# A megakernel of two transformer-like layers: 39 expert tiles, bias additions moved, the front of layer 1 a step sooner, the last quad in halves

## The chip, the cores and the metric

The kernel runs on one NeuronCore of one Trainium2 chip. The metric is the device time of one execution in microseconds; lower is better.

## The reference, cut to what matters

Two layers, each x + attention(xn) + ffn(xn), with xn the layer norm of x. x is 8 x 256 x 128 in float32, that is 2048 tokens in 16 tiles of 128.

```python
x = L0_attn_x
xn = _layernorm(x)
x = x + _L0_attn_ref(xn, ...) + _L0_ffn_ref(xn, ...)
xn = _layernorm(x)
x = x + _L1_attn_ref(xn, ...) + _L1_ffn_ref(xn, ...)
return x

# layer 0, attention: linear, 4 heads of 32
k = softmax(k, axis=1); context = einsum('bnhd,bnhe->bhde', k, v)
out = einsum('bhde,bnhd->bnhe', context, q) @ w_out + b_out; return out + x
# layer 0, ffn: 8 experts, each token goes to the best 2 by a router
h = u * silu(gate)          # [u, gate] = xn @ w_up[e].T, hidden 256
out = sum_k weight_k * (h_k @ w_down[e_k].T); return out + skip
# layer 1, attention: 16 heads of 64, q and k to unit length, 2 null keys,
# ALiBi slopes, causal mask, softmax; out @ w_out
# layer 1, ffn: 8 experts, grouped top 2 of a softmax router, hidden 256
```

## The kernel before

**Layer 0.** After the norms and the router, VectorE works out for each of the 4096 (token, expert) pairs a place in a list sorted by expert, each expert's part filled up to whole tiles of 128 places. At most 2 x 16 + 8 - 1 = 39 tiles are in use; the kernel handles 40 of them (`SLOTS`) in 20 pairs (`PAIRS`). `sources` turns the list into row numbers for the gathers, `slots` names each tile's expert. For each pair s, GpSimd issues two indirect DMAs (`pair_rows`, `sorted_tile`, line 505) into one of four rooms, so the gather of pair s waits for the transpose of pair s-4. TensorE's queue has, for each s in this order: the up products of pair s (six matmuls, lines 1483 to 1485, `pair_ups`), the transpose of the gathered rows of pair s+2 (`pair_turn`, line 1584), the down products of pair s-2 (line 1624), the transposes of the hidden rows of pair s-1 (line 1613). ScalarE and VectorE split the turned rows into a high and a low part, and do the gate. Between the gathers of pairs 5 to 8 and the next ones GpSimd does `output_bias`, an addition of the output bias to four tiles of the accumulator (line 500). SyncE stores each pair's results.

The attention of layer 0 is done by `mixing`, in ticks: in tick t the products of q and k of batch t, the rest of the batches before it. Ticks 0 to 5 stand behind the pairs, ticks 6 to 12 at steps of layer 1 listed in `MIX_AT` (line 383).

**Layer 1** is one sequence of steps s = -16 to 134, written out for each engine by `all_steps`. In step k (0 to 127) the scores of head pair k mod 8 of a query tile are computed (line 1812), biased on VectorE (line 1426), taken to the exponential on ScalarE (line 877); one step later the probabilities are turned (line 1876), three steps later multiplied with the values (line 1827). Four steps make a quad: a reciprocal and a product with it on VectorE (line 1412, `norm`), four transposes to `b_y` (line 1847), a copy (line 1468), eight passes of the output product (line 1798) and the addition to the accumulator (line 1449), at 7, 8, 8 and 10 steps behind the quad's first.

The `front` prepares q and k of the next batch in 8 pieces, two steps apart: projection (`PROJ_AT` = -9, lines 1483 to 1485, to the bank `b_front`), copy and square on ScalarE (lines 801, 805), sum on VectorE (line 1362, at -8), root on GpSimd (line 577, at -7), product with the root (line 318, -6, on VectorE for batches 0 and 7), transposes back to `b_front` (line 1690, `TURN_AT` = -4), copy on ScalarE (line 817). The scores of step 0 wait for two turned pieces.

`x1(b)` adds the rows that the experts of layer 0 gave (fetched by `take_rows(b)`, four gathers on GpSimd, line 544) to batch b's accumulator (line 1206) and takes the statistics, `row_roots` (line 552) their root on GpSimd, `x1_normal` and `x1_rhos` what follows on VectorE. For batch 1: x1 at step -5, root at -4, the rest at 1; `take_rows(2)` stands at step 0, `take_rows(3)` at step 3.

Each engine takes its instructions in order; a wait on a semaphore holds up all that is behind it on its engine.

## Time and profile before

| | |
|---|---|
| median of 3 runs | 642.15 us (641.12 to 643.76) |
| the profiled execution, its own time | 641.26 us |
| its span, first to last instruction | 639.4 us |
| TensorE matmul busy | 560.4 us, 88% of the span |
| ScalarE / VectorE / GpSimd busy | 432.4 / 423.9 / 351.1 us |
| mean granted TensorE clock | 0.983 of full |

The profile gives for each engine its busy time; a timeline of instructions with start, duration, line, operation, tiles written and read, and in brackets how long the engine was idle before and what released it; and tables of busy time for stretches of the span, with the clock that TensorE was granted (1.00 is 2.4 GHz, 0.50 is 1.2 GHz). Rough stages: norms, router and sorting until 44 us; expert pairs 44 to 120; mixing and the opening of layer 1 until 158; steps of layer 1 until 628; tail.

### The profile page before, as it was taken

How to read it: one execution, taken by the hardware profiler on the slowest of the kernel's cores; microseconds unless marked ns; L12 is line 12 of the kernel's file. 1: busy time of each engine (PE TensorE's matmuls, PEld its weight loads, DVE VectorE, ACT ScalarE, POOL GpSimd, SP SyncE). 2: the span in 40 equal slices, each digit the busy share in tenths (PEclk: the TensorE clock that was granted, in tenths of full speed). 3: DMA queues.
4: the chain of work that ended last, by engine and by line, in shares of the span. 5: the costliest groups of instructions: out<-in, count | busy, mean ns of one | idle time of the engine just before them, and what ended most of it. 6: DMA issues, size and time to landing. Idle time of an engine off the chain costs nothing.

```text
span 639.4 us, 13356 instructions
## 1 busy us (share of the span) xinstructions
PE 560.4 (88%) x3760; PEld 440.5 (69%) x3760; DVE 423.9 (66%) x1531; ACT 432.4 (68%) x1200; POOL 351.1 (55%) x302
## 2 busy tenths in 40 slices
PE   2417899986999988898999999999999999999797
PEld 1406688774767767666777777777777777777576
DVE  5785855475788776889756665566565665587663
ACT  3724786444877878676677777777777776887552
POOL 3617874235888696435564634554454443688800
PEclk9999999997799999999999999999999999999898
DMA  8602234410111013000000100100011100112200
GB/s 309 221 8 55 69 94 75 140 59 1 34 34 30 6 34 100 0 2 2 14 17 27 26 23 22 29 23 22 23 30 30 22 14 10 30 51 58 64 5 10
DMA packets 26326, 29.13 MB, mean 46 GB/s; under 512 B 3920, under 2 KB 22384, under 8 KB 25744
## 3 DMA queue, kind: packets, MB, share of 16 engines
q1 hardware_dynamic: 21680, 18.89, 9.4%
q0 software_dynamic: 4576, 9.38, 6.5%
q8 instruction: 35, 0.57, 0.4%
q14 instruction: 35, 0.29, 0.1%
HBM read 19.94 MB, written 8.32 MB: 44 GB/s over the span
## 4 chain that ended last, share of the span: by engine, by line
PE 58%; DVE 17%; POOL 11%; issue 9%; ACT 3%; DMA 2%; SPq 0%; POOLq 0%; DVEq 0%; ACTq 0%
PE b_last L1827 8%; PE b_upB L1812 7%; POOL taken L628 4%; PE b_rest L1876 4%; PE b_upB L1798 4%; PE b_last L1690 3%; PE b_rest L1665 3%; POOL moe_buf L505 3%; PE b_last L1483 2%; PE b_upA L1745 2%; PE b_upA L1483 2%; POOL rn L577 2%; PE b_rest L1847 2%; PE b_rest L1624 2%; PE b_upA L1484 2%
## 5 line engine op out<-in xcount | busy, mean ns | idle before, releaser
L877 ACT ACTIVATE prb<-prb,mneg 128x130 f32<-128x130 f32 (+1 forms) x256 | 114.7, 449 | 93.6 <-DVE mneg L1426 93.1
L577 POOL TENSOR_TENSOR rn<-ss,halves 128x8 f32<-128x8 f32 x64 | 107.4, 1679 | 97.0 <-DVE ss L1364 96.3
L1426 DVE CUSTOM_DVE_ANT_0 prb<-b_upB,bias 128x130 f32<-128x130 f32 (+1 forms) x256 | 81.5, 356 | 113.7 <-PE b_upB L1812 113.4
L505 POOL DMA_INDIRECT moe_buf<-normal_rows,source x79 | 79.7, 1009 | 93.1 <-PE b_rest L1779 62.9
L1827 PEld LDWEIGHTS b_last<-v,prT_all 128*128 128x128 f32 x768 | 100.1, 192 | 15.1 <-DVE qs_all L1412 8.7
L1827 PE MATMUL b_last<-v,prT_all 128*128 128x64 f32 x768 | 101.5, 268 | 5.6 <-DVE qs_all L1412 5.6
L1812 PE MATMUL b_upB<-qkT 64*128 64x258 f32 (+1 forms) x512 | 78.2, 383 | 0.2 <-DVE pnT L1436 0.2
L886 ACT ACTIVATE prT_all<-b_rest 128x512 f32<-128x512 f32 (+1 forms) x128 | 61.3, 479 | 6.8 <-PE b_rest L1876 6.2
L1876 PE MATMUL b_rest<-cst,prb 128*128 128x128 f32 x384 | 63.5, 274 | 0.0
L1876 PEld LDWEIGHTS b_rest<-cst,prb 128*128 128x128 f32 x384 | 47.7, 150 | 17.7 <-issue 17.6
L1812 PEld LDWEIGHTS b_upB<-qkT 64*128 64x128 f32 x512 | 39.4, 188 | 23.6 <-issue 18.5
L318 POOL TENSOR_TENSOR qk<-qk,rn 128x512 f32<-128x512 f32 x48 | 50.8, 1059 | 3.8
L877 ACT ACTIVATION_READ_ACCUMULATOR prb<-prb,mneg 128x1 f32 x256 | 47.8, 187 | 0.0
L1690 PE MATMUL b_last<-cst,qk 128*128 128x128 f32 x256 | 43.6, 295 | 3.9 <-DVE qk L318 3.0
L1362 DVE TENSOR_REDUCE ss<-sq 128x8 f32<-128x512 f32 x64 | 43.3, 676 | 4.0 <-ACT sq L805 3.7
L544 POOL DMA_INDIRECT taken<-expert_rows,pos x32 | 31.6, 988 | 22.4 <-DMA expert_rows<-moe_buf 13.9
L1798 PE MATMUL b_upB<-wout,oT 128*128 128x128 f32 x256 | 36.0, 285 | 6.8 <-DVE mneg L1426 6.0
L805 ACT ACTIVATE sq<-qk 128x512 f32<-128x512 f32 x64 | 40.4, 631 | 2.1
L1690 PEld LDWEIGHTS b_last<-cst,qk 128*128 128x128 f32 x256 | 28.5, 146 | 17.8 <-issue 7.8
L801 ACT ACTIVATE qk<-b_last 128x512 f32<-128x512 f32 x64 | 37.0, 577 | 4.6 <-PE b_last L1485 4.6
L1798 PEld LDWEIGHTS b_upB<-wout,oT 128*128 128x128 f32 x256 | 31.8, 196 | 9.4 <-issue 8.8
L628 POOL DMA_INDIRECT taken<-expert_rows,pos x32 | 33.1, 1033 | 8.8 <-issue 8.8
(330 smaller groups left out, 1272.2 us busy)
## 6 DMA issues: line engine op xcount, KB each, us to landing
expert_rows<-moe_buf SPq DMA_DIRECT2D x20, 128.0 KB, 1.9
expert_rows<-moe_buf SPq DMA_DIRECT2D x39, 64.0 KB, 1.5
bias<-w_up SPq DMA_DIRECT2D x1, 2048.0 KB, 9.5
down<-w_dn SPq DMA_DIRECT2D x2, 1024.0 KB, 10.6
moe_buf<-w_up SPq DMA_DIRECT2D x4, 512.0 KB, 4.1
moe_buf<-normal_rows,source POOLq DMA_INDIRECT x79, 2.6
qk<-x SPq DMA_DIRECT2D x8, 128.0 KB, 4.1
v<-w_qk SPq DMA_DIRECT2D x1, 1024.0 KB, 12.2
```

Source lines behind the costliest of these rows:

```text
L318: engine.tensor_tensor(part, part, norms.unsqueeze(2).to_broadcast([P, HALF, DH1]), ALU.mult).then_inc(unit, 1)
L505: nc.gpsimd.indirect_dma_start(out=room, out_offset=None, in_=normal_rows[layer], in_offset=bass.IndirectOffsetOnAxis(ap=source[layer][:, ...
L577: nc.gpsimd.tensor_tensor(rn[hs], ss[hs], halves[:], ALU.pow).then_inc(pool_root, 1)
L628: nc.gpsimd.indirect_dma_start(out=taken_rows[b % 2][:, t, k], out_offset=None, in_=expert_rows, in_offset=bass.IndirectOffsetOnAxis(ap=po ...
L877: nc.scalar.activation(prb[k % 3][:, i, 0:n], prb[k % 3][:, i, 0:n], ACT.Exp, scale=-1.0, bias=mneg[:, qt, h:h + 1], accum_out=lsum[:, qt, ...
L886: nc.scalar.activation(prT[k % 3][:, :, 0:n], b_prT[:, 0:2 * n].rearrange("p (a n) -> p a n", a=2), ACT.Copy).then_inc(act_prT, 1)
L1426: nc.vector.tensor_tensor_reduce(prb[k % 3][:, i, 0:n], b_sim[i][:, 0:n], bias[:, h, KEYS - n:KEYS], 1.0, FMAX, ALU.add, ALU.min, mneg[:, ...
L1690: ins = nc.tensor.transpose(b_front[:, i * P:(i + 1) * P], qk[:, w, t, hp * P:(hp + 1) * P], ident)
L1798: ins = nc.tensor.matmul(b_op, oT[:, a], wout1[:, m % 2 * 4 + a], start=(a == 0), stop=(a == 3))
L1812: nc.tensor.matmul(b_sim[i][:, 0:n], qT[ch, hp, toks], kT[ch, hp, 0:n], start=True, stop=True).then_inc(pe_sim, 1)
L1827: ins = nc.tensor.matmul(b_pv[:, at:at + DH1], prT[k % 3][:, i, c * P:(c + 1) * P], v[:, c, h * DH1:(h + 1) * DH1], start=(k % 4 == 0 and ...
L1876: ins = nc.tensor.transpose(b_prT[:, (i * nc1 + c) * P:(i * nc1 + c + 1) * P], prb[k % 3][:, i, NULL + c * P:NULL + (c + 1) * P], ident)
```

## The change

1. Layer 0 handles 39 tiles: the last pair has one tile in its gather, its transpose, its up, hidden and down work on TensorE. Operations of ScalarE and VectorE still treat both halves.
2. `output_bias` stands behind all gathers on GpSimd. `sources` stands ahead of `slots` on VectorE.
3. TensorE's turn of pair 1 stands behind the up products of pair 0.
4. In layer 1 the first four turns of the front go to the bank `b_pv` a step sooner, and don't wait for the projections; projections up to piece 6 don't wait for a turn's copy. Mixing ticks 9 to 12 stand at steps -7, -6, -5, -4 instead of -9, -8, -7, -6. For batch 1, x1 stands at step 1, its root at 2, the rest at 3.
5. Last quad (31): product, transposes and copy in two halves each, the second half turned to `b_front`. Quad 30: transposes at 7 instead of 8 steps behind, output product at 11 instead of 10.

```diff
+        EARLY_TURNS = 4
+        def turn_bank(m):
+            return b_pv if m < EARLY_TURNS else b_front
+        def turned_at(s):
+            return [m for m in piece_at(s, TURN_AT) if m >= EARLY_TURNS] + [m for m in piece_at(s, TURN_AT - 1) if m < EARLY_TURNS]
+        LAST = 4 * B - 1
+        def outputs_at(s):
+            return [m for m in quad_at(s, 8) if m != LAST - 1] + [m for m in quad_at(s, 7) if m == LAST - 1]
+        def projected_at(s):
+            return [m for m in quad_at(s, 10) if m != LAST - 1] + [m for m in quad_at(s, 11) if m == LAST - 1]
+        def turned_bank(a, m):
+            return b_y if m < LAST else (b_front if a else b_y)[:, 0:2 * P]
+        def parts_out(m):
+            return [(0, 2), (2, 4)] if m == LAST else [(0, 4)]
...
-        MIX_AT = [-STEPS, -11, -10, -9, -8, -7, -6]
+        MIX_AT = [-16, -11, -10, -7, -6, -5, -4]
...
+        def parts_of(s):
+            return range(2 if s < PAIRS - 1 else 1)
...
-                for t in range(2):
+                for t in parts_of(s):
                     sorted_tile(0, s, 2 * s + t, rows_in[s % 4][:, t], rows_loaded[s % 4])
...
                 pair_rows(s)
-                if 5 <= s < 9:
-                    output_bias(4 * (s - 5))
...
+            for at in range(0, TILES, 4):
+                output_bias(at)
...
-                if s == -4:
-                    row_roots(1)
...
+                if s == 2:
+                    row_roots(1)
...
+            sources(0)
             slots(0)
-            sources(0)
...
-                if s == -5:
+                if s == 1:
                     x1(1)
                     x1_variances(1)
-                if s == 1:
+                if s == 3:
                     x1_rhos(1)
                     x1_normal(1)
...
+                    for a, e in parts_out(m):
+                        cols_of, heads = slice(a * P, e * P), slice(2 * a, 2 * e)
+                        nc.vector.tensor_tensor(o_half[m % 2][:, cols_of]...,
+                                                b_pv[:, cols_of]...,
+                                                heads8[:, heads]..., ALU.mult).then_inc(dve_norm, 1)
...
-            pe.wait_ge(*ROUTED("source"))
+            pe.wait_ge(*ROUTED("slots"))
             load_experts(0)
...
-            for s in range(2):
-                pair_turn(s)
+            pair_turn(0)
             for s in range(PAIRS + 2):
                 if s < PAIRS:
                     pair_ups(s)
+                if s == 0:
+                    pair_turn(1)
...
-                    if m > 2:
+                    if m > EARLY_TURNS + 2:
                         pe.wait_ge(act_turn, m - 2)
...
-                    pe.wait_ge(act_proj, min(m + 3, 8 * B))
+                    if m == 0:
+                        pe.wait_ge(mix_dve["add"], mix_bank.index(b_pv) + 1)
+                    elif m >= EARLY_TURNS:
+                        pe.wait_ge(act_proj, min(m + 3, 8 * B))
```

## Rows read from the trace of the kernel before

**Rows 1.** Windows: stretch, length, busy of PE, PEld, DVE, ACT, POOL, granted clock, DMA.
```profile
440.00:460.00 20.00, 20.00 (x146) 16.27 (x145) 12.38 (x45) 15.20 (x45) 8.40 (x8) 1.00 0.09 22
149.00:155.00 6.00, 2.30 (x10) 1.09 (x8) 5.46 (x18) 3.35 (x6) 3.47 (x3) 0.84 0.00 0
...
161.00:164.00 3.00, 2.81 (x11) 1.78 (x9) 2.41 (x13) 2.05 (x7) 2.67 (x3) 0.50 0.26 67
...
167.00:170.00 3.00, 3.00 (x24) 2.36 (x22) 1.11 (x7) 2.67 (x8) 2.39 (x3) 1.00 0.18 44
```

**Rows 2.** Timeline (start, duration, engine, line, operation, idle before), TensorE in the pairs.
```profile
61.95 0.38 PE L1584 MATMUL b_last<-cst,moe_buf 128*128 128x128 f32 x2
...
73.95 0.44 PE L1584 MATMUL b_last<-cst,moe_buf 128*128 128x128 f32 x2 [1.19 <-DMA moe_buf<-normal_rows,source]
...
87.32 0.38 PE L1584 MATMUL b_last<-cst,moe_buf 128*128 128x128 f32 x2
...
104.78 0.40 PE L1485 MATMUL b_upA<-up_h,xa_l 128*128 x1
105.02 0.38 PE L1584 MATMUL b_last<-cst,moe_buf 128*128 128x128 f32 x2
105.24 1.06 PE L1624 MATMUL b_rest<-down,moe_buf 128*128 x8
```

**Rows 3.** Timeline, GpSimd in the pairs: bias addition, gathers, the operation behind the gathers.
```profile
59.55 1.29 POOL L500 TENSOR_TENSOR acc_all<-acc_all,small 128x512 f32<-128x512 f32 x1
...
68.38 1.77 POOL L505 DMA_INDIRECT moe_buf<-normal_rows,source  x1 [0.16 <-issue]
70.45 0.94 POOL L505 DMA_INDIRECT moe_buf<-normal_rows,source  x1 [0.30 <-issue]
...
106.19 2.38 POOL L532 TENSOR_TENSOR nvbd<-taken,nvbd 16x1024 fp32r<-16x1024 f32 x1 [4.35 <-issue]
```

**Rows 4.** Timeline, the last source matmul and the source cast.
```profile
42.27 0.32 PE L1560 MATMUL b_rest<-moe_buf,th 128*128 128x40 f16 x4 [0.29 <-DVE th L1055]
...
43.25 0.18 DVE L1065 CAST source<-b_rest 128x40 uint32<-128x40 f32 x1
```

**Rows 5.** Timeline, VectorE beside bias additions and without one.
```profile
66.85 2.46 DVE L1142 TENSOR_TENSOR wqk_l<-v,wqk_h 128x1024 fp32r<-128x1024 f32 x1
...
71.60 0.69 DVE L1173 TENSOR_TENSOR th<-b_upB,th 128x512 f32<-128x512 f32 x1
...
72.53 1.27 DVE L1142 TENSOR_TENSOR wqk_l<-v,wqk_h 128x1024 fp32r<-128x1024 f32 x1
```

**Rows 6.** Timeline, the opening: x1 of batch 1, turn 1, projection 4, first scores.
```profile
151.13 1.25 DVE L1206 SCALAR_TENSOR_TENSOR acc_all<-taken,half_share,acc_all 128x128 f32<-128x128 f32 x4
...
155.05 1.08 PE L1690 MATMUL b_last<-cst,qk 128*128 128x128 f32 x4 [1.60 <-DVE qk L318]
...
157.01 0.76 PE L1483 MATMUL b_last<-wqk_h,xa_h 128*128 128x512 f32 x1 [0.87 <-ACT qkT L817]
...
158.55 0.81 PE L1812 MATMUL b_upB<-qkT 64*128 64x130 f32 x4
```

**Rows 7.** Timeline, GpSimd in the first steps of layer 1.
```profile
158.17 1.02 POOL L544 DMA_INDIRECT taken<-expert_rows,pos  x1 [0.17 <-issue]
...
162.98 1.68 POOL L577 TENSOR_TENSOR rn<-ss,halves 128x8 f32<-128x8 f32 x1
...
166.24 1.46 POOL L544 DMA_INDIRECT taken<-expert_rows,pos  x1 [0.30 <-issue]
```

**Rows 8.** Timeline, the tail: output products, product with the reciprocals, last addition.
```profile
630.12 1.11 PE L1798 MATMUL b_upB<-wout,oT 128*128 128x128 f32 x8
...
632.45 0.69 DVE L1412 TENSOR_TENSOR qs_all<-b_last,rl 128x512 f32<-128x512 f32 x1 [0.79 <-DVE rl L1407]
...
634.69 2.04 PE L1798 MATMUL b_upB<-wout,oT 128*128 128x128 f32 x8 [0.83 <-issue]
636.77 0.29 DVE L1449 TENSOR_TENSOR acc_all<-b_upB,acc_all 128x128 f32<-128x128 f32 x1 [2.18 <-PE b_upB L1798]
```

More of the change, by code:

```diff
@@ L369, in build @@
         PLACES = ["both", "rank", "before", "fill", "ntile", "upto", "base", "first", "place", "own0", "own1", "posf0", "posf1", "pos",
-                  "lane", "tile", "where", "marked", "past", "slotf", "slots", "source"]
-        routes = [progress("route0", ["lg", *FIRST(0), "rest", *FIRST(1), "gap", *PLACES, "den", "w0", "w1", "share"]),
+                  "lane", "tile", "where", "marked"]
+        SLOTTED = ["past", "slotf", "slots"]
+        routes = [progress("route0", ["lg", *FIRST(0), "rest", *FIRST(1), "gap", *PLACES, "source", *SLOTTED, "den", "w0", "w1", "share"]),
                   progress("route1", ["lg", "top", "shift", "sum", "rsum", "prob", "grp", *FIRST("g0"), "grest", *FIRST("g1"), "gmask", "masked",
-                                      *FIRST(0), "rest", *FIRST(1), *PLACES, "den", "rden", "share"])]
+                                      *FIRST(0), "rest", *FIRST(1), *PLACES, *SLOTTED, "source", "den", "rden", "share"])]
         def ROUTED(name, layer=0):
@@ L398, in build @@
         pair_h, pair_l = (xa_h, xf_h), (xa_l, xf_l)
+        def parts_of(s):
+            return range(2 if s < PAIRS - 1 else 1)
+        PAIRS_LOADED = [sum(16 * len(parts_of(s)) for s in range(i, PAIRS, 4)) for i in range(4)]
         def pair_th(s):
@@ L805, in front @@
                     nc.scalar.activation(sq[:], part, ACT.Square).then_inc(act_sq, 1)
-                for m in piece_at(s, TURN_AT):
+                for m in turned_at(s):
                     b, n = divmod(m, 8)
@@ L1578, in pair_turn @@
             def pair_turn(s):
-                pe.wait_ge(rows_loaded[s % 4], 32 * (s // 4 + 1))
+                pe.wait_ge(rows_loaded[s % 4], sum(16 * len(parts_of(i)) for i in range(s % 4, s + 1, 4)))
                 if s >= 2:
                     pe.wait_ge(pair_dve["xl"], s - 1)
-                for t in range(2):
+                for t in parts_of(s):
                     ins = nc.tensor.transpose(pair_T[s % 2][:, t * P:(t + 1) * P], rows_in[s % 4][:, t], ident)
@@ L1610, in pair_hidden @@
                     pe.wait_ge(pair_act["hidT"], s)
-                for t in range(2):
+                for t in parts_of(s):
                     for a in range(HB):
@@ L1796, in scores @@
                         pe.wait_ge(dve_add, m)
-                    for a in range(4):
-                        ins = nc.tensor.matmul(b_op, oT[:, a], wout1[:, m % 2 * 4 + a], start=(a == 0), stop=(a == 3))
+                    for i, (first, end) in enumerate(parts_out(m)):
+                        pe.wait_ge(dve_oT, m + 1 + i)
+                        for a in range(first, end):
+                            ins = nc.tensor.matmul(b_op, oT[:, a], wout1[:, m % 2 * 4 + a], start=(a == 0), stop=(a == 3))
                     ins.then_inc(pe_op, 1)
```

44 lines of the change are left out of this document (24 added, 20 removed).

## The prediction

> **What bounds the kernel now.** I read the windows of 20 us first, then the chain that ended last, then the timeline where that chain leaves TensorE. From 200 us on there is nothing to find for this change: between 440 and 460 us TensorE is busy for all 20 us [rows 1], and that window stands for those around it, from 300 to 580 us. None of the edits takes work out of that stretch, so whatever is won before it shifts it as a block, and the gain can only lie in three places in which TensorE waits: the expert pairs of layer 0 (44 to 120 us), the opening of layer 1 (143 to 200 us), and the tail (after 628 us).
>
> In the pairs, the last TensorE step of a period is the transpose of the gathered rows (line 1584). One period without waits takes (105.02 - 87.32) / 6 = 2.95 us; but from the transpose of pair 5 to that of pair 12 it is 87.32 - 61.95 = 25.37 us for seven, 4.72 us more than 7 x 2.95 = 20.65, and the transpose of pair 8 alone sat idle 1.19 us for its gather [rows 2]. GpSimd explains it: a gather costs 0.95 us and 0.30 us until the next, so 2.5 us for a pair, less than TensorE's 2.95; but with a bias addition of 1.29 us and 0.16 us before the next gather a pair costs 4.0 us, and there are four such pairs [rows 3]. In the opening, TensorE is busy only 2.30 of 6 us before 155 us, its granted clock then stands at 0.50 (1.2 GHz), and the chain goes around from square to sum, root, product, transpose and copy, one piece at a time [rows 1, 6]. The tail is a serial walk through one quad: the product with the reciprocals, four transposes, a copy, eight matmul passes at half clock [rows 8].
>
> **The gathers (bias behind them, source before slots).** Four additions of 1.29 + 0.16 us leave the gather queue: 5.8 us. They run after the last gather, where GpSimd idled 4.35 us before its next operation [rows 3] and the bias is first read by the mixing's additions in its fifth tick, after the last pair: price nothing; if that cover were gone it would be 5.8 us. The source cast no longer stands behind the three slot operations: it began at 43.25 us, while the last matmul it needs runs from 42.27 for 0.32 us [rows 4]; with some 0.1 us for the hand-over the first gather starts 0.55 us sooner. The slots are read by TensorE only before the first up product, 5 us later: price nothing.
>
> GpSimd and VectorE also get in each other's way. Of two equal vector operations the one at 66.85 us, beside a bias addition, took 2.46 us, the other 1.27, and the gather begun at 68.38 us, before the first of them ended, took 1.77 instead of 0.94 [rows 3, 5]. So the move also frees VectorE about 1.2 us there, while the gathers still lose 0.8 us twice. A vector operation with a PSUM operand was not slowed (0.69 us at 71.60 us beside a bias addition [rows 5]), and these are the ones that the additions will now stand beside.
>
> What is late next: the second gather of pair 5 stands right before the first addition, so it began near 58.6 us and now begins at 58.0. Six pairs of 2.52 us later, with 0.8 us twice and the small power that GpSimd does at pair 9 (an estimate, 0.9 us, as much as a gather), the second gather of pair 11 is issued at 75.6 us and, with the 3.5 us that pair 8 took from issue (70.45) to transpose (73.95) [rows 2, 3], is there at 79.1. TensorE, free of waits from pair 5 at 61.4, wants it at 61.4 + 6 x 2.95 = 79.1. So it catches up just about: pair 12 comes at 82.1 to 82.7 instead of 87.32. I take 5.0 us for the two edits; bounds 3 (gathers still hold two or three pairs by 0.7 us each) and 5.3.
>
> **The first up products between two turns.** They can start 1.7 us sooner, as soon as pair 0 is split, but the next thing in TensorE's queue is the transpose of pair 2, whose gather lands when it landed before (less the 0.55 above). ScalarE's queue has the input of pair 1 ahead of the gate of pair 0, and both are done by then. Nothing, between 0.3 us lost and 0.5 won.
>
> **39 tiles.** The 40th slot is always empty. In the last pair three up matmuls go (0.23 us each, as from 104.78 to 105.02), one transpose of two (0.11, half of 105.02 to 105.24), two of four hidden transposes (0.22 by the same row), and half of the eight passes of the down product, about 0.5 of its 1.06 [rows 2]. The up and the transpose are on TensorE's path (0.8); after that the chain goes over ScalarE and VectorE, whose operations still treat both halves, and the mixing, which starts between the last two down products, gains the 0.22 and perhaps some of the rest. I take 1.1 us, bounds 0.8 and 1.4. The gather less on GpSimd is worth nothing, as it is ahead by then.
>
> **The front of layer 1.** Before, turn 0 waits for three projections and the next projection for the copy of the turn, because all share one bank; now the first four turns go to another bank one step sooner, and the mixing ticks 9 to 12 stand later. I followed the queues with the durations of before, on its time scale. VectorE no longer has x1 of batch 1 between the sum of piece 2 and the product of piece 1: its four multiply-adds alone are 1.25 us from 151.13, with statistics and variances 2.2. Against that, the sums now stand ahead of the mixing's vector work in VectorE's queue, the last mixing products wait for it, and the third projection behind them comes some 0.8 us later. So turn 1 starts about 1.8 us sooner than 155.05, if half of that delay lies on the path. From there to the first scores it was 158.55 - 155.05 = 3.5 us: a turn at half clock of 1.08, a copy, and a projection from 157.01, which waited for the copy. Now the projection follows the turn at once (0.7 each at full clock, half of what they took), and turn 2 stands between them and the scores, with its wait for the root: 2.6 us. Together the first scores come 1.8 + 0.9 = 2.7 us sooner, at 155.9 [rows 6].
>
> Then the moved work asks for it back. x1(1) stands in step 1, on VectorE between the first steps of attention, its roots on GpSimd in step 2 and its normalisation in step 3. GpSimd is the queue behind which this matters: four gathers (5 us) in step 0, a root of 1.68 us, four gathers again in step 3, with no gap but its own 0.2 to 0.3 us of issue from 158.17 us on [rows 7]. It begins 1.8 us sooner now, but takes the root operation of 1.0 us too (before in a gap), and root 5, behind the second four, for which VectorE and with it all later steps wait, ends 1.8 - 1.0 = 0.8 to 1.1 us sooner. Part of that wait was VectorE's own work (the x1 normalisation in step 1, which now falls later), so of the 2.7 us I leave 1.4. Upper bound 2.7, nothing given back; lower bound a loss of 1.0: x1(1) wholly on the path (2.1 us) and the root besides, against those 2.1 saved ahead.
>
> A row speaks against the move: the gather at 166.24 us took 1.46 instead of 0.95 us [rows 7] while x1 operations with their operands in SBUF ran, and x1(1) now lies beside gathers; one such stretch costs 0.5 us, within the bounds. The Trainium skill says so (GPSIMD Engine Reference, 8. Key points): GpSimd shares its SBUF interfaces with VectorE, and contention comes with vector instructions that have two SBUF inputs or run in a two-port mode. By that rule x1(1) would also hold up the gathers of step 0, and the front would gain 0.9 instead of 1.4 us.
>
> **The tail.** The output product of quad 30 moves from before the last value products to behind them. It stood from 630.12 to 631.2 on TensorE's full queue, so the product with the reciprocals (632.45) comes 0.95 us sooner [rows 8]; the moved one then runs while VectorE works on the first half. The transposes of quad 30 move ahead by a step, within a full queue: nothing. Then halves: before, from the start of the reciprocal product to the last addition it is 636.77 - 632.45 = 4.32 us. Now, from 631.5: half products until 631.9 and 632.3, transposes of the first half behind the moved product, at 632.2, of the second at 632.5, copies of 0.41 us until 633.1 and 633.5, and the output product from 633.1. At half clock its eight passes take 2.04 us [rows 8], that is an end at 635.2 (gain 1.5); at full clock, with the 1.11 of the row at 630.12, 634.1 (gain 2.7). The shorter idle times make the latter possible for a part. I take 2.0; three more vector instructions and three more waits are in it.
>
> **Sum.** 5.0 + 0 + 1.1 + 1.4 + 2.0 = 9.5 us. The profiled execution: span 639.4 us, its own time 641.26, so 1.86 us lie around the span, and it is 0.9 us under the median of 642.15. Span 629.9, own time 631.8, median 632.7 us.
>
> **Rivals.** (a) The pairs stay paced by gathers: landing times of 3.5 us and the held gathers eat the lead, since TensorE asks for each pair 0.1 us before it is there; for it the small margin, against it that TensorE caught up before although four additions stood in between. Pairs give 2.5 less: 635.2. (b) The opening gives nothing or turns into a loss of 1 us: VectorE, in order, carries x1(1) after the scores have begun and its root sits behind four gathers. 634 to 635.1. (c) More than I say: the front keeps all of its 2.7 us and the tail its 2.7: 630.7, and with the clock at full speed in the stretch of 155 to 167 us, which TensorE filled at 0.50 [rows 1], another 2: 628.7. (d) Slower than before: TensorE waits more often in steps 1 to 5, as VectorE and GpSimd pace them, and its clock stays at the lower level beyond 167 us. The output product shows the price: 2.04 us at half clock against 1.11 at full [rows 8]. A stretch full of TensorE's work gives back half of its length; from 19 us of further half clock the 9.5 us are gone, and with 30 us the time is 632.7 + 15 = 647.7. The rows say that TensorE came back to full speed by 167 us with only such work, so little speaks for it. The Trainium skill (TensorE: Matmul & The Clock Gate, Part 1) has the slow clock as the default state that activity releases, which is what would carry this rival. (e) The shift doesn't travel: something at a fixed time, such as the weights of layer 1, holds the block. They are asked for after the last pair's rows, so they move too. If all but the tail were lost: 640.
>
> **Chances.** Forecast (630.5 to 634) 0.50; (a) 0.12; (b) 0.15; (c) 0.15; (d) 0.04; (e) 0.04. Range 629.0 to 637.5: it takes in (a) and (b), most of (c) and leaves out (d), (e). A measurement of this kernel can tell 0.5% (3.2 us) from no change. Faster by more: 0.91, within: 0.05, slower by more: 0.04.
>
> **What would show it.** The gathers in an unbroken row from 0.55 us sooner on with the four additions behind the last; the transpose of pair 12 near 82.4; the first mixing product 6 us sooner; the first scores 8 to 9 us sooner than 158.55, and step 16 about 7.5 us sooner; the granted clock back at 1.00 by step 4; from the last value product to the last addition about 4 us. I am wrong if a transpose after pair 9 still waits over 0.5 us, if step 16 is less than 6.5 us sooner, or if the shift changes between steps 16 and 120.

## The result, and the profile after

The changed kernel takes 636.59 us (median of 5 runs, 635.75 to 637.03) beside 641.33 us for the kernel before on the same chip: the ratio is 0.9922, interval 0.9906 to 0.9937. It is 0.8% faster, 4.7 us. That lies inside the stated range (629.0 to 637.5), but the forecast gain was 9.5 us, so half of it is missing. The profiled execution has a span of 634.4 us (before 639.4), 636.22 us of its own, and a mean granted clock of 0.997; the four others had 0.991 or 0.992, so the profile shows less time at half clock than they had.

I cut the span into stretches by marks that both traces have: the start of the first gather of layer 0, the first transpose behind the mixing (line 1742 after), the start of VectorE's bias addition (line 1462) of steps 0, 16, 48, 104 and 127, and the start of the last addition. Lengths in us:

| stretch | before | after | difference |
|---|---|---|---|
| start to first gather | 44.31 | 43.73 | -0.58 |
| first gather to mixing | 92.78 | 91.21 | -1.57 |
| mixing to step 0 | 22.42 | 19.84 | -2.58 |
| step 0 to step 16 | 49.63 | 50.49 | +0.86 |
| step 16 to step 48 | 111.76 | 111.66 | -0.10 |
| step 48 to step 104 | 232.68 | 234.18 | +1.50 |
| step 104 to step 127 | 72.69 | 72.52 | -0.17 |
| step 127 to last addition | 10.5 | 8.2 | -2.3 |

The front (-1.7 up to step 16) and the tail (-2.3) came as forecast. The pairs gave 2.15 us with the 39 tiles instead of 6.1, and a stretch in which I had seen nothing to find lost 1.5.

Timeline of the changed kernel, GpSimd and VectorE where the gathers begin (start, duration, engine, line, operation, idle before):
```profile
42.64 0.20 DVE L1098 CAST source<-b_rest 128x40 uint32<-128x40 f32 x1 [0.41 <-PE b_rest L1596]
43.73 1.20 POOL L538 DMA_INDIRECT moe_buf<-normal_rows,source  x1 [16.22 <-DVE slotf L1106]
43.86 2.46 DVE L985 SCALAR_TENSOR_TENSOR up_l<-bias,small,up_h 128x1024 fp32r<-128x1024 f32 x2
45.23 1.92 POOL L538 DMA_INDIRECT moe_buf<-normal_rows,source  x1 [0.30 <-issue]
47.46 0.95 POOL L538 DMA_INDIRECT moe_buf<-normal_rows,source  x1 [0.30 <-issue]
```
and the same place in the kernel before:
```profile
43.36 2.46 DVE L952 SCALAR_TENSOR_TENSOR up_l<-bias,small,up_h 128x1024 fp32r<-128x1024 f32 x2
44.31 1.39 POOL L505 DMA_INDIRECT moe_buf<-normal_rows,source  x1 [16.82 <-DVE source L1065]
46.01 0.95 POOL L505 DMA_INDIRECT moe_buf<-normal_rows,source  x1 [0.31 <-issue]
47.27 0.95 POOL L505 DMA_INDIRECT moe_buf<-normal_rows,source  x1 [0.30 <-issue]
```
The cast is 0.61 us sooner than in [rows 4] and the first gather 0.58. But the split of the up weights (two operations, 2.46 us) now starts behind the slots, and the second gather starts while the second of them runs. That operation ends at 46.32, the gather at 47.15: 1.92 us instead of 0.95. The third gather starts 0.2 us later than before.

Timeline of the changed kernel, TensorE in the first pairs:
```profile
50.55 0.79 PE L1519 MATMUL b_upA<-up_h,xa_h 128*128 x1 [1.02 <-DVE xa_l L1197]
...
53.27 0.63 PE L1620 MATMUL b_last<-cst,moe_buf 128*128 128x128 f32 x2
55.31 0.69 PE L1620 MATMUL b_last<-cst,moe_buf 128*128 128x128 f32 x2 [1.41 <-DMA moe_buf<-normal_rows,source]
55.65 0.78 PE L1519 MATMUL b_upB<-up_h,xf_h 128*128 x1
```
and in the kernel before:
```profile
51.07 0.69 PE L1584 MATMUL b_last<-cst,moe_buf 128*128 128x128 f32 x2 [1.72 <-DMA moe_buf<-normal_rows,source]
51.98 0.63 PE L1484 MATMUL b_upA<-up_l,xa_h 128*128 x1
55.46 0.40 PE L1484 MATMUL b_upB<-up_l,xf_h 128*128 x1
```
The up products of pair 0 now come ahead of the transpose of pair 1, which started at 51.07 before and starts at 53.27 now; pair 1's split and gate follow later. The products of pair 0 take 0.63 us apiece (the first of a group more), as they did before. Those of pair 1 take 0.63 as well, where they took 0.40 before. 0.63 is what a product of the same size takes where the granted clock reads 0.50 (291 us in "after again" below). The tables print 1.00 for these microseconds, but that is no reading: the trace holds its first record of the clock at 59.4 us (54.1 in the kernel before), and a stretch without a record counts as 1.00. In all 14 traces the up products take 0.63 us until that first record and 0.40 behind it. So TensorE worked at the lower level until 59.4 us here; it had idled 6.27 us before the transpose of pair 0 (6.10 before the change).

Timeline of the changed kernel, TensorE and ScalarE around pair 9, and GpSimd behind the gathers:
```profile
72.03 3.20 ACT L757 ACTIVATE nvbd<-taken 16x1024 fp32r<-16x1024 f32 x3
72.73 0.38 PE L1620 MATMUL b_last<-cst,moe_buf 128*128 128x128 f32 x2
75.26 0.60 ACT L771 ACTIVATE th<-b_upA 128x512 f32<-128x512 f32 x1
75.68 0.38 PE L1620 MATMUL b_last<-cst,moe_buf 128*128 128x128 f32 x2
77.04 1.15 PE L1660 MATMUL b_rest<-down,moe_buf 128*128 x8 [0.98 <-ACT moe_buf L778]
79.86 0.27 PE L1620 MATMUL b_last<-cst,moe_buf 128*128 128x128 f32 x1
...
82.81 0.38 PE L1620 MATMUL b_last<-cst,moe_buf 128*128 128x128 f32 x2
...
96.26 5.03 POOL L533 TENSOR_TENSOR acc_all<-acc_all,small 128x512 f32<-128x512 f32 x4
101.69 2.38 POOL L565 TENSOR_TENSOR nvbd<-taken,nvbd 16x1024 fp32r<-16x1024 f32 x1 [0.40 <-POOL acc_all L533]
```
No transpose behind pair 2 has a gather as its releaser for more than the hand-over; pairs follow in 2.95 us from 60.92 on. One interval is 4.18 instead of 2.95: ScalarE copies the null values for 3.20 us, a gate waits behind them in its queue until 75.26, and the down product 0.98 us for what follows from it. The four additions stand behind the last gather. GpSimd's next operation now starts 5.46 us behind that gather's end, where it was 4.35, so they outlast their gap by 1.1 us; but behind it GpSimd idles 16.08 us until the rows that it fetches next are there, so nothing is lost. Pair 12 comes at 85.76, 1.56 us sooner than in [rows 2].

Windows of the changed kernel (columns as in [rows 1]), the opening and the full stretch, then the timeline of its tail:
```profile
149.00:155.00 6.00, 3.37 (x21) 2.11 (x19) 3.58 (x8) 4.76 (x8) 4.12 (x3) 1.00 0.00 0
158.00:164.00 6.00, 4.74 (x31) 3.08 (x27) 4.77 (x26) 4.29 (x14) 5.19 (x6) 1.00 0.13 33
440.00:460.00 20.00, 19.77 (x141) 15.83 (x139) 12.62 (x48) 15.26 (x46) 10.66 (x9) 1.00 0.07 18
```
```profile
628.40 0.47 PE L1878 MATMUL b_last<-nvbd,pnT 96*128 96x512 f32 x1
628.97 0.76 DVE L1447 TENSOR_TENSOR qs_all<-b_last,rl 128x256 f32<-128x256 f32 x2 [1.24 <-issue]
630.43 0.41 DVE L1504 COPY oT<-b_last 128x256 f32<-128x256 f32 x1
630.66 1.13 PE L1839 MATMUL b_upB<-wout,oT 128*128 128x128 f32 x8 [0.45 <-DVE oT L1504]
631.83 0.29 DVE L1485 TENSOR_TENSOR acc_all<-b_upB,acc_all 128x128 f32<-128x128 f32 x1 [0.98 <-PE b_upB L1839]
```
In the opening TensorE works 3.37 of 6 us where it had 2.30 [rows 1], and the granted clock never leaves 1.00. From the product with the reciprocals to the last addition it is 2.86 us, not 4.32 [rows 8], with the output product at full clock (1.13 against 2.04).

### The profile page after: what moved, and what is told of

It is laid out like the page before. It is cut to its first block, busy times and chain, and to the rows that moved or that the text cites. A ratio compares the mean times of both kernels' runs of the same rounds, so it can differ in the third digit from the quotient of the medians.

```text
span 634.4 us, 13326 instructions
## 1 busy us (share of the span) xinstructions
PE 554.3 (87%) x3750; PEld 438.1 (69%) x3750; DVE 421.1 (66%) x1533; ACT 430.8 (68%) x1200; POOL 348.2 (55%) x301
## 4 chain that ended last, share of the span: by engine, by line
PE 62%; DVE 16%; issue 9%; POOL 8%; ACT 3%; DMA 2%; SPq 0%; POOLq 0%; DVEq 0%; ACTq 0%
PE b_last L1870 9%; PE b_upB L1853 8%; PE b_rest L1920 5%; PE b_upB L1839 4%; POOL taken L661 4%; PE b_last L1730 3%; PE b_rest L1702 3%; PE b_rest L1660 3%; PE b_upA L1519 2%; POOL rn L610 2%; PE b_last L1519 2%; PE b_upA L1785 2%; PE b_upA L1520 2%; PE b_upA L1521 2%; PE b_rest L1891 2%
## 5 line engine op out<-in xcount | busy, mean ns | idle before, releaser
L538 POOL DMA_INDIRECT moe_buf<-normal_rows,source x78 | 77.9, 999 | 94.7 <-PE b_rest L1819 63.1
L919 ACT ACTIVATE prT_all<-b_rest 128x512 f32<-128x512 f32 (+1 forms) x128 | 61.4, 480 | 8.2 <-PE b_rest L1920 7.7
L1920 PEld LDWEIGHTS b_rest<-cst,prb 128*128 128x128 f32 x384 | 47.4, 150 | 17.8 <-issue 16.4
L1853 PEld LDWEIGHTS b_upB<-qkT 64*128 64x128 f32 x512 | 39.1, 185 | 25.0 <-issue 17.8
L1730 PE MATMUL b_last<-cst,qk 128*128 128x128 f32 x256 | 42.0, 287 | 4.1 <-DVE qk L318 2.4
L1504 DVE COPY oT<-b_rest 128x512 f32<-128x512 f32 (+1 forms) x32 | 21.9, 683 | 25.0 <-PE b_rest L1891 25.0
```

The costliest lines, as they stand in the source:

```text
L538: nc.gpsimd.indirect_dma_start(out=room, out_offset=None, in_=normal_rows[layer], in_offset=bass.IndirectOffsetOnAxis(ap=source[layer][:, ...
L919: nc.scalar.activation(prT[k % 3][:, :, 0:n], b_prT[:, 0:2 * n].rearrange("p (a n) -> p a n", a=2), ACT.Copy).then_inc(act_prT, 1)
L1730: ins = nc.tensor.transpose(turn_bank(m)[:, i * P:(i + 1) * P], qk[:, w, t, hp * P:(hp + 1) * P], ident)
L1853: nc.tensor.matmul(b_sim[i][:, 0:n], qT[ch, hp, toks], kT[ch, hp, 0:n], start=True, stop=True).then_inc(pe_sim, 1)
L1920: ins = nc.tensor.transpose(b_prT[:, (i * nc1 + c) * P:(i * nc1 + c + 1) * P], prb[k % 3][:, i, NULL + c * P:NULL + (c + 1) * P], ident)
```

## The experiments

Three chips served; each ratio is against the kernel before on the same chip (medians 641.57, 651.13 and 641.29 us in the three groups). The changed kernel itself ran beside the others in the third group only, so in the first two a median is set against it by way of its ratio, 0.9922, and the intervals mostly overlap. There the stretches of the traces carry the argument, not the medians. Lengths of the stretches defined above, in us, with the time at a granted clock of 0.50 that lies in each:

| kernel | gather to mixing | mixing to 16 | 16 to 48 | 48 to 104 | tail |
|---|---|---|---|---|---|
| before | 92.78 | 72.05 (13.7 us at 0.50) | 111.76 | 232.68 | 10.5 |
| after | 91.21 | 70.33 | 111.66 | 234.18 | 8.2 |
| bias only | 89.49 | 71.58 (13.7) | 112.87 (3.4) | 232.97 | 9.96 |
| turns first | 89.48 | 71.25 (10.2) | 112.71 (3.4) | 234.44 | 8.2 |
| turns, null | 88.48 | 70.33 | 112.71 (3.4) | 234.28 | 8.2 |
| turns, null, slots | 87.37 | 72.42 (10.2) | 114.09 (twice 3.4) | 234.32 | 8.2 |
| after again | 90.52 | 70.30 | 112.71 (3.4) | 234.28 | 8.2 |
| norm first | 89.40 | 71.56 (10.2) | 112.66 (3.4) | 233.07 | 8.2 |
| four edits | 87.58 | 70.30 (3.4) | 114.07 (twice 3.4) | 233.28 | 8.2 |
| four, no front | 87.36 | 71.59 (13.7) | 114.10 (twice 3.4) | 233.14 | 8.2 |

Between steps 104 and 127, which the table leaves out, all of them have a stretch at 0.50 near 600 us. It lasts 3.4 us and the steps take 72.5 to 72.7 us, except in "turns first" and "turns, null, slots": there it lasts 6.8 us and they take 73.5 and 73.4.

### First group: the pairs

**b1_bias_only**, the kernel before with one edit:
```diff
                 pair_rows(s)
-                if 5 <= s < 9:
-                    output_bias(4 * (s - 5))
...
+            for at in range(0, TILES, 4):
+                output_bias(at)
             for i in range(4):
                 pool.wait_ge(rows_loaded[i], PAIRS_LOADED)
```


> The kernel before with one edit: the four bias additions stand behind all gathers. Theory T: from the transpose of pair 5 to that of pair 12 the 25.37 us become 20.65 and 1.2 us for the null value copies that come into the open, a gain of 3.5 us, 637.8 us against 641.3. Rival R4 (what was forecast: gathers alone, nothing behind them): 4.4 us or more. Rival R5 (the gathers still pace, by their own 2.52 us and their landing): under 2 us.

638.29 us (637.75 to 638.85), ratio 0.9949, interval 0.9932 to 0.9965. Gather to mixing is 3.29 us shorter, and the seven pairs of 25.37 us take 21.91. This one edit alone brings 3.3 of the changed kernel's 4.7 us. Its trace has the same gap at pair 9 (4.20 us):
```profile
70.00 3.21 ACT L724 ACTIVATE nvbd<-taken 16x1024 fp32r<-16x1024 f32 x3
...
75.02 1.15 PE L1624 MATMUL b_rest<-down,moe_buf 128*128 x8 [0.97 <-ACT moe_buf L745]
```
So the null values' cost belongs to the moved additions, not to another edit; before, ScalarE ran the same copies at 71.88 us, when TensorE stood waiting for a gather (1.19 us for pair 8 [rows 2]), and no wait on TensorE named them.

**e1_turns_first**, the changed kernel with the first two transposes ahead of the loop again:
```diff
-            pair_turn(0)
+            for s in range(2):
+                pair_turn(s)
             for s in range(PAIRS + 2):
                 if s < PAIRS:
                     pair_ups(s)
-                if s == 0:
-                    pair_turn(1)
```


> The changed kernel with one edit undone: both first transposes stand ahead of the up products of pair 0 again. Theory T (the earlier start thins out TensorE's work, so its clock stays at half until 58.8 us and pair 1's six up products take 0.63 instead of 0.40 us each): the transpose of pair 3 comes near 57.0 instead of 58.36 us, everything behind it is 1.3 us sooner, 635.3 us. Rival R1 (the late gather of pair 2, at 55.3 us in the changed kernel, sets the pace, whatever stands before it): under 0.3 us, 636.4 us.

637.46 us (634.97 to 640.52), ratio 0.9937, interval 0.9918 to 0.9957. The mark of the mixing comes 1.6 us sooner than after (133.31 against 134.94), and pair 3 is transposed at 57.23 instead of 58.36. But the order alone isn't what costs. The three executions of the first and third group with the changed order took 91.21, 90.52 and 89.40 us from gather to mixing, against 89.48. In the last of them the ups of pair 1 already ran at full speed:
```profile
54.76 0.44 PE L1620 MATMUL b_last<-cst,moe_buf 128*128 128x128 f32 x2 [1.21 <-DMA moe_buf<-normal_rows,source]
54.95 0.48 PE L1519 MATMUL b_upB<-up_h,xf_h 128*128 x1
55.27 0.40 PE L1520 MATMUL b_upB<-up_l,xf_h 128*128 x1
```
(timeline of the kernel "norm first" below). All 14 traces sort themselves by this. From the last source matmul to the transpose of pair 4 it is 16.6 to 17.2 us in the seven kernels with the old order, even where pair 1's products were slow ("four edits", 16.90). With the new order it is 16.6 to 16.9 in the three traces with fast products in pair 1 (the kernel with the front back, the one with the null values later, and "norm first") and 17.8 to 18.6 in the four with slow ones. The new order costs 1 to 1.8 us when TensorE's clock rises late, and nothing when it rises before pair 1's products. By the first clock record it rose at 54.1 to 57.0 us with the old order, and at 53.8 to 54.4 or at 58.0 to 59.4 with the new one.

The median is no better than that of the changed kernel, though: in its profile 0.9 us are gone again by step 16, with 10.2 us at half clock in the opening, 1.05 us between steps 16 and 48, and 0.97 between 104 and 127.

**e3_turns_null**, the same with the null values' three copies at pairs 14, 15 and 16:
```diff
-                if s == 5:
-                    null_values()
+                if 14 <= s < 17:
+                    null_values(NULL_PARTS[s - 14])
```


> As the run before, and ScalarE's three null value copies (3.2 us, in one piece at pair 5) are spread over pairs 14 to 16. Theory T (with the gathers ahead of TensorE, the gate of pair 7 waits for these copies, and TensorE with it, 1.2 us at pair 9): the interval of 4.18 us between the transposes of pairs 9 and 10 becomes 2.95, another 1.2 us, 634.1 us. Rival R2 (they only fill a gap of ScalarE, and the gathers of pairs 9 and 10 are as late): under 0.3 us.

635.0 us (633.57 to 638.6), ratio 0.991, interval 0.9884 to 0.9936. Every interval from pair 4 on is 2.95 us, and gather to mixing is 1.0 us shorter than with the turns alone.

**e4_slots_first**, the same with the slots ahead of the sources:
```diff
-            sources(0)
             slots(0)
+            sources(0)
```


> As the run before, and the slot operations stand ahead of the source cast again, as in the kernel before the change. Theory T (the cast 0.6 us sooner wins nothing, because VectorE's two splits of the up weights, 2.46 us, now lie beside the first two gathers, the second of which takes 1.92 us): the first gather starts 0.6 us later, the gathers of pair 1 on as early or 0.2 us sooner, total 0.2 us less to 0.1 us more. Rival R3 (an earlier source is an earlier pair): 0.6 us more.

635.5 us (633.54 to 638.66), ratio 0.9894, interval 0.9871 to 0.9917. The first gather is 0.5 us later (44.43), the second takes 0.95 us instead of 1.93, the third is sooner (47.38 against 47.65), and from the last source matmul to the mixing it is 89.40 us instead of 89.92. Not all of that is the order's. In this run only the first of pair 1's up products was still slow, in the run before the first three. Between traces roughly alike in that, the transpose of pair 4 stands 0.27 us sooner with the slots first ("turns first" 16.92 against 16.65 here; "turns, null" 17.17 against 16.90 in "four edits"). So putting the sources first, for which I had counted 0.55 us won, cost about 0.3, and the clock the rest. The median, 0.5 us above that of the run before, can't show it: the executions lie between 633.5 and 638.7.

### Second group: the other parts

The chip of this group was slow in one place: between 64 and 67 us all engines waited in all four kernels for something that the trace doesn't name (ScalarE sat idle for 6.5 us), and shorter waits of this kind follow. The median of the kernel before is 9.8 us above that of the first comparison. Only stretches after it are compared.

**f3_40_tiles**, the changed kernel with the empty tile of the last pair again, and **f2_tail_back**, with the whole output part as before:
```diff
         def parts_of(s):
-            return range(2 if s < PAIRS - 1 else 1)
+            return range(2)
```
```diff
         def outputs_at(s):
-            return [m for m in quad_at(s, 8) if m != LAST - 1] + [m for m in quad_at(s, 7) if m == LAST - 1]
+            return quad_at(s, 8)
...
-                for m in outputs_at(s):
+                for m in quad_at(s, 8):
+                    pe.wait_ge(dve_norm, m + 1)
                     pe.wait_ge(act_v, min(m + 2, 4 * B))
```


> The changed kernel with 40 tiles in layer 0: the last pair has its empty tile again. T (1.1 us forecast for the tile, all of it on the way to the mixing): the first mixing product 1.0 to 1.1 us later than in the changed kernel, at 116.2, median 637.7. R (the mixing takes only what the last up matmuls and transposes save, and layer 1 swallows it): first mixing product 0.8 us later, median 636.6 to 637.1.

648.43 us (645.54 to 651.84), ratio 0.9966, interval 0.9934 to 0.9998. From the transposes of pair 18 to the mark behind the mixing it is 32.07 us with 40 tiles (this kernel and the one before) and 31.39 to 31.46 with 39; to the second group of mixing products (line 1562) 14.24 against 13.22. The tile is worth 1.0 us on TensorE, but 0.6 at the mark.

> The changed kernel with the text of the output part put back: the last quad whole, its neighbour's transposes and product at their old steps, and the order of the waits on TensorE and VectorE as before. T (the tail is worth 2.2 us and nothing else hangs on it): median 638.8, the lead over the kernel before at step 104 as in the changed kernel, 2.5 us, and the last four steps of the kernel 10.4 us long as before. R2 (the order of the waits, which runs 32 times in layer 1, costs some 0.05 us each time): the lead at step 104 stays at 3.9 us, that of step 48, and the median is 637.2 to 637.5.

647.43 us (645.05 to 648.96), ratio 0.9934, interval 0.9906 to 0.9962. The tail is 9.58 us instead of 8.19. So the edit of the tail brings 1.4 us where the whole output product ran at full clock (here, 1.13 us), 1.8 against the bias-only kernel (1.52 us) and 2.3 against the profile before (2.04 us). But the medians hardly differ, since steps 48 to 104 take 233.12 us here and 234.0 to 234.6 in the other three of the group: the loss in the middle of layer 1 comes with the text of the output part.

**f1_front_back**, the changed kernel with the front of layer 1 as before (early turns, mixing ticks, x1 of batch 1 and its roots):
```diff
-        EARLY_TURNS = 4
+        EARLY_TURNS = 0
...
-        MIX_AT = [-16, -11, -10, -7, -6, -5, -4]
+        MIX_AT = [-STEPS, -11, -10, -9, -8, -7, -6]
```


> The changed kernel with its front of layer 1 put back: turns in the shared bank at their old steps, mixing ticks, x1 of batch 1 and its roots at their old steps. T (the front is worth what was forecast, 1.4 us, and what shrinks the lead later in layer 1 comes from elsewhere): median 1.4 us above the changed kernel's 636.6, so 638.0; the first step of attention 2.6 us later than in the changed kernel, step 16 about 1.5 later, and the lead over the kernel before still shrinks by about 1.5 us between steps 48 and 104. R1 (the front brings the later loss with it): the lead stays constant after step 48, and the median is 636.6 or under (635.5 to 636.6).

648.03 us (646.47 to 651.51), ratio 0.9947, interval 0.9917 to 0.9978. Mixing to step 0 takes 22.8 us against 21.2 to 22.1, but up to step 16 it is 72.7 against 72.8 to 73.6: nothing was gained on this chip, where all four had 6.8 to 13.7 us at half clock in the opening. In all three groups the four traces without the new front have 13.7 us at half clock there and the ten with it 0 to 10.2. Steps 48 to 104 still take 234.58 us: the loss there isn't the front's.

**e2_null_later**, the changed kernel with the null values' copies at pairs 14 to 16 (the diff above) and nothing else:

> The changed kernel with one edit: ScalarE's three copies of the null values, 3.2 us in a row at pair 5, go one each to pairs 14, 15 and 16. T (they hold up the gate of pair 7 and so the down product by 1.2 us, now that gathers no longer cover it): the interval of 4.18 us between two pair transposes becomes 2.95, the mixing starts 1.2 us sooner, and the median is 635.4 to 635.6. R (the lead is given back at the opening of layer 1, whose roots and gathers pace it): the mixing 1.2 sooner, but the median 636.2 to 636.6.

645.81 us (645.0 to 652.3), ratio 0.9925, interval 0.9894 to 0.9956, the lowest median of the group, by 1.6 us. The gap of 4.18 us at pair 9 is 2.95 here, so the edit does what it should, though no difference of the medians is clear of the spread; two others of 4.3 us stand elsewhere in its pairs, as gaps of 4.3 to 4.8 us do in all four kernels of this group.

### Third group: the loss in the middle of layer 1

I summed the time from each TensorE instruction to the next over steps 56 to 104. In the bias-only kernel and the changed one every sum agrees within 0.1 us except one: from the last value product to the first of the four output transposes, 12 times, 3.64 us in all against 4.73. The four kernels of the second group split the same way (3.68 with the output part as before, 4.57 with 40 tiles). What arrives last at that place is not the normalised output but VectorE's split of the tile. The kernel before waited for the output first and for the split last; the changed one, whose halves needed the wait inside the loop, waits for the output last.

**g0_after_again** is the changed kernel itself; **g1_norm_first** has one edit:
```diff
                 for m in outputs_at(s):
+                    pe.wait_ge(dve_norm, m + 1)
                     pe.wait_ge(act_v, min(m + 2, 4 * B))
...
-                        pe.wait_ge(dve_norm, m + 1 + i)
+                        if i:
+                            pe.wait_ge(dve_norm, m + 1 + i)
```


> The changed kernel itself, as the measure for the three that run beside it. On a chip like that of the first comparison 636.6 us against 641.3. In its trace the transition from the last value product of a quad to the first of the four output transposes takes 0.395 us on average over steps 56 to 104, as it did there.

636.69 us (634.07 to 636.9), ratio 0.9917, interval 0.9896 to 0.9937; the transition takes 4.79 us in 12.

> The changed kernel with one edit: ahead of the output transposes TensorE waits for the normalised output first and for the split of the tile last, as before the change. T (the changed order costs 91 ns in each of the 12 quads between steps 56 and 104, because what arrives last there is the split of the tile, and another wait now stands behind it): the lead over the kernel before no longer shrinks between steps 48 and 104, beyond the 0.3 us it shrank by with the bias edit alone, and the median is 1.1 us under that of the changed kernel in this call. R (the drift comes with the other edits of the output part, the waits of the copy on VectorE or of the product): the same 0.395 us, the same drift of 1.5 us, no difference in the median.

635.23 us (633.79 to 637.05), ratio 0.9904, interval 0.9884 to 0.9925. The transition is back at 3.67 us in 12, and steps 48 to 104 take 233.07 us instead of 234.28. The timeline shows it, first the changed kernel, then this one:
```profile
437.73 0.28 DVE L1407 TENSOR_TENSOR xf_l<-b_rest,xf_h 128x128 fp32r<-128x128 f32 x1
438.23 0.42 PEld L1891 LDWEIGHTS b_rest<-cst,qs_all 128*128 128x128 f32 x4
```
```profile
436.96 0.28 DVE L1407 TENSOR_TENSOR xf_l<-b_rest,xf_h 128x128 fp32r<-128x128 f32 x1
437.36 0.42 PEld L1893 LDWEIGHTS b_rest<-cst,qs_all 128*128 128x128 f32 x4
```
From the start of the split to the weight load: 0.50 us with another wait behind the late one, 0.40 with none. The normalised output had been done 6.4 us before the split began. The 91 ns are a mean over the 12 quads, not the same in each: the changed kernel takes 0.1 us more in most of them and up to 0.27 in one, in every fourth quad both orders take 0.50, and in the last one both take 3.3. The intervals of the two medians overlap; the stretch of the trace is what decides.

**g2_four_edits** is the changed kernel with turns first, null values later, slots first and this order of waits; **g3_no_front** is the same without the front of layer 1.

> The changed kernel with four edits: both first pair transposes ahead of the first up products, the null values' copies at pairs 14 to 16, the slots before the sources, and the order of waits of the run beside it. T (the costs add: 1.4 to 1.6 for the first, 1.2 for the second, 0.3 to 0.6 for the third, 1.1 for the fourth, less up to 1.5 that the opening of layer 1 takes back when its granted clock falls): median 2.5 to 4 us under that of the changed kernel in this call, 632.5 to 634. R (the opening's clock takes all of it but the wait order): 1.1 us under.

634.77 us (632.38 to 636.88), ratio 0.989, interval 0.9865 to 0.9915: 1.9 us under the changed kernel, where 2.5 to 4 was expected. Gather to mixing is 2.9 us shorter than in the run of the changed kernel beside it and steps 48 to 104 take 1.0 less, but steps 16 to 48 are 1.4 us longer. Windows of this kernel and of the changed one in its second run:
```profile
246.00:248.00 2.00, 1.66 (x12) 1.57 (x13) 1.90 (x10) 2.00 (x7) 1.64 (x1) 1.00 0.03 8
248.00:251.50 3.50, 3.50 (x17) 2.71 (x16) 1.18 (x2) 2.24 (x4) 3.40 (x2) 0.52 0.00 0
```
```profile
285.00:290.00 5.00, 3.58 (x27) 2.24 (x26) 5.00 (x10) 3.20 (x10) 3.99 (x3) 1.00 0.02 5
290.00:295.00 5.00, 4.87 (x25) 4.41 (x27) 4.35 (x12) 2.69 (x7) 3.72 (x3) 0.66 0.01 2
```
Where the router of layer 1 leaves TensorE gaps, the clock falls to half for 3.4 us, and the traces with such a fall are 1.0 to 1.4 us longer for each (111.6 to 111.8 us in the six without, 112.7 to 112.9 in the five with one, 114.1 in the three with two). The kernel before has none of these in its profile, each of the kernels of the first and third group has one or two, and the first run of the changed kernel and the four traces of the second group had none.

> The run beside it (four edits) with the front of layer 1 put back as before the change. T (the front is worth 1.4 us as forecast): median 1.4 us above the four edits. R (the front makes the opening faster when TensorE's granted clock stays at full there, by 1.6 us, and slower when it doesn't, since TensorE then idles more often between pieces): median within 0.5 us of the four edits, and a granted clock of 0.50 in 150 to 180 us in the profile of one or both.

635.87 us (633.25 to 636.22), ratio 0.99, interval 0.9879 to 0.9921: 1.1 us above the four edits, within the spread. In the traces the front is worth 1.29 us from the mixing to step 16 (71.59 against 70.30), here with 13.7 us at half clock in the opening without it and 3.4 with it.

## Why the prediction was right and wrong

**The gathers: 5.0 us forecast for both edits, 3.3 measured for the additions and 0.3 lost by the sources.** The mechanism of the additions held: they stand behind the gathers, the gathers come in an unbroken row, VectorE's operation is no longer doubled. The step that failed is "TensorE, free of waits from pair 5". I compared the gathers only with TensorE's own period and didn't ask what else had been late in those 4.7 us. ScalarE's null values were: 3.2 us in one queue with the gate. They cost TensorE 1.2 us as soon as gathers no longer covered them (bias-only, and the removal in the turns-null kernel). This is what is late next, which my text named a gather. In the changed kernel pair 5 was transposed at 63.88 us, not at 61.4 as I had it, which comes from the next two points.

**Source before slots: 0.55 us won by the forecast, 0.3 lost by the measurement.** I priced the cast and put the slots at nothing, but they push VectorE's long split by 0.5 us. The second gather then starts while it runs and takes 1.92 us instead of 0.95. I had the price of such a meeting in [rows 3, 5] and didn't apply it here. The Trainium skill (GPSIMD Engine Reference, 8. Key points) says that GpSimd and VectorE share interfaces to SBUF and contend when vector instructions read two operands there; the split does, and the trace agrees with these 1.92 us.

**Ups between turns: nothing forecast, 0 to 1.7 us lost.** My argument was that the next transpose waits for its gather anyway. That looked at pair 2 and left out two things: pair 1, whose transpose moved from 51.07 to 53.27 behind six products of 0.63 us, and TensorE's clock. Where it rises only behind pair 1's products, these take 0.63 us instead of 0.40 as well, and the new order has no gap left that takes up the delay. With the clock up by then it cost nothing, so the bounds (0.3 lost to 0.5 won) fit one of the two cases. What makes the rise come earlier or later is not shown: two kernels with the same text in this part, the tail back and the front back, have it at 58.5 and at 53.8 us.

**39 tiles: 1.1 forecast, 0.6 to 1.0 measured.** The working was right for TensorE (1.0 to the second mixing product); at the mark behind the mixing only 0.6 were left. The bounds were 0.8 and 1.4.

**Front: 1.4 forecast, 1.7 measured from the mixing to step 16,** and 1.3 where two kernels differ by the front alone. The first scores are 2.58 sooner (forecast 2.7), given back to 1.5 by step 5, where GpSimd's roots stand behind the gathers. The gain goes with the clock, as in rival (d) but smaller: with 10.2 us at half clock in the opening at most 0.3 us of the front's gain are left by step 16 (71.25 with "turns first", 71.56 with "norm first", 72.42 with "turns, null, slots", against 71.59 without the front), and the second group shows none. By the Trainium skill (GPSIMD Engine Reference, 8. Key points) I had x1 of batch 1 holding up gathers as a possibility. Here the measurement decides against it: x1's operations began at 157.18 us, and the gathers at 157.06 and 158.31 took 0.94 us each. I had also misread [rows 7]: what ran beside the gather of 1.46 us at 166.24 wasn't x1 but the product with the roots:
```profile
166.20 0.68 DVE L318 TENSOR_TENSOR qk<-qk,rn 128x512 f32<-128x512 f32 x1
```

**Tail: 2.0 forecast, 2.3 measured in the profile.** The new product ran at full clock (1.13 us), for which I had worked out 2.7. 0.9 of the 2.3 us are that clock (1.13 against 2.04); the halves and the moved product by themselves bring the other 1.4, as the tail-back kernel shows. That kernel's product ran at full clock too, so the shorter idle times, to which I had put this clock, aren't shown to be its reason.

**"Shifts it as a block": wrong.** Two of my own marks of being wrong came true: the shift changes between steps 16 and 120, and step 16 is 3.9 us sooner (205.27 against 209.14), not 6.5 or more. 1.2 us are the order of waits ahead of the output transposes, which the halves changed for all 32 quads; I had put the tail's edit in the tail alone. The remaining 0.3 us are lost in the bias-only kernel as well. The unchanged windows at full TensorE hid it: 20.00 of 20 us busy in [rows 1] is the modelled end of matmuls, and 91 ns between two of them don't show there.

Added up for the profiled pair: 0.6 + 1.6 + 2.6 - 0.9 + 0.1 - 1.5 + 0.2 + 2.3 = 5.0 us, the difference of the spans. The time lies inside the stated range because the range took in rivals (a) and (b), and neither is what happened: gathers no longer paced the pairs, and the opening gained. That the losses which I hadn't seen fit into that margin is luck. What stays open: when the clock rises in the first pairs, what makes it fall near 290 us in the shifted kernels and not in the one before (TensorE has the same gaps there in both), and what held up the chip of the second group at 64 us.

## What to carry to other kernels

When a wait is taken away, list every queue that was late during it, not only the one that ended it: the second latest sets the new time. An edit made for the last iteration runs in all of them; look where its text stands, and put the wait that arrives last also last in the program. Stretches at half clock came and went between executions and kernels here and went with about 1 us each, as much as an edit brings, so read a gain of a few us stage by stage and not from the median alone. And a clock that a view prints as 1.00 is worth a check against the durations of equal products.

## What the hardware showed that I had not expected

A satisfied wait behind the one that arrives last isn't free on TensorE: 91 ns on average over 12 quads, mostly 0.50 against 0.40 us from the start of the split to the weight load.

An indirect gather on GpSimd that starts while VectorE runs a long operation with two operands in SBUF ends 0.8 to 0.9 us behind the end of that operation, however long that takes. This held for the splits of the query and key weights (128x1024, 1.2 us, or 2.46 beside a bias addition) and the products with the roots (128x512, 0.7 us) in all 14 traces, and for the second operation of the split of the up weights: 1.77 us at 68.38 and 1.46 at 166.24 in the kernel before, 1.92 at 45.23 in the changed one. Only the gather that starts beside the first of those two ends 1.1 us behind its end (1.39 us at 44.31). Two gathers that started 0.03 us ahead of a product took their 0.94 us, and the first gather of the changed kernel, 0.13 us ahead of the split, took 1.20. Beside x1's operations of 128x128, which take 0.3 us each, a gather took 0.94 to 1.10 us.

TensorE's up products take 1.6 times as long in the first pairs (0.63 against 0.40 us), until 53.8 to 59.4 us by the trace. A fall of the granted clock to half for 3.4 us goes with 1.0 to 1.4 us in a stretch in which TensorE has gaps.
